# Router logits of a mixture of experts computed with the weights stationary, and an order of work changed with them

## The chip, the core and the metric

The kernel runs on one core of a Trainium2 chip. Its engines work side by side and meet only at semaphores: TensorE (PE, with its weight loads shown apart as PEld), VectorE (DVE), ScalarE (ACT), GpSimd (POOL) and the DMA queues, of which SyncE (SP) issues many. The metric is the time of one execution in microseconds (us), lower is better.

## The reference

A graph layer, a linear attention and a mixture of experts follow each other over 3125 tokens of 256 features. What the change touches is the router at the head of the experts:

```python
logits = tokens @ router_w.T                 # (3125, 256) x (256, 8), float32
probs = softmax(logits); rw, re = top_k(probs, 2); rw = rw / rw.sum(-1)
out = tokens
for e in range(8):
    out = out + combine[:, e:e+1] * (gelu(tokens @ w1[e] + b1[e]) @ w2[e] + b2[e])
```

The tokens here are the layer-normalised sum of the input, the graph layer and the attention.

## The kernel before

The 3125 tokens are 25 tiles of 125 rows, handled in 5 groups of 5 tiles. After the graph and attention part (which ends at about 315 us) comes the router stage, and after that the experts, in 64 chunks of 128 rows that each belong to one expert: 32 chunks for the tokens' first choice (rank 0), 32 for their second (rank 1). A token's row reaches its place in the table of chunks (`xs`, in DRAM) by an indirect DMA that GpSimd issues, one for each tile and rank: `send(t, r2)`, 25 for rank 0 and 25 for rank 1. SyncE loads the first chunk only when all 25 rank 0 sends have landed, and the padding rows of all eight experts too (`store_pad`, issued by SyncE and ScalarE once the counts are known).

The order of work is written out by hand, one program for each engine. For group g:

- TensorE: `graph3(g)` (the last product of the graph layer, five matmuls), `transpose_tokens(g)`, `logits(g)`, `positions(g)` (places of the tokens in their experts' lists).
- VectorE: `add_graph(g)` (adds the graph layer's result, then the variance, signalled as `var2_done`), `scale(g)`, `choose(g)` (the two best experts), `weigh(g)` (the places, signalled as `slot_done`).
- ScalarE: `token_scale(g)` (a square root, with a table load ahead of it for all groups but two), `normalize_tokens(g)`, an exponential for the two weights, `copy_tokens(g)` (transposed tokens out of PSUM).
- GpSimd: for each group, after its `slot_done`, five rank 0 sends and `BETWEEN` rank 1 sends; behind the last group's five, rank 1 sends up to number `EARLY`; the remaining rank 1 sends go between the experts' stores.

VectorE's loop matters for the change and is left as it is by it:

```python
for g in range(G):
    if g + 1 < G:
        scale(g + 1)
    choose(g)
    if g + 2 < G:
        add_graph(g + 2)
    weigh(g)
```

`add_graph(g)` begins by waiting for `graph3(g)`, `positions(g)` on TensorE waits for `weigh(g - 1)`, and `scale(g)` waits for `token_scale(g)`, which waits for `add_graph(g)`.

Of the kernel before, what the change touches and what calls it, by code (L numbers as in the profile page):

```python
# [14 lines left out]
TP = 125  # L15
NT = N // TP
J = 5
G = NT // J
EC = NE // TP
P = 128  # L20
H1, H2 = 64, 32
NX = 8
# [14 lines left out]
NBLK = len(BLOCKS)  # L37
HALF_TILES = 12
MC = 32
BETWEEN, EARLY = 2, 15  # L40
XB = 6
NCH = 2 * MC
CAP = N + P + 3
# [1 line left out]
RR = NX * CAP + NULLS * P  # L45
NOWHERE = 4096.0
CTX0 = 128
assert NG == NB * TP and GT * W == TP and NE % TP == 0


def build(nc, a, out):
# [3 lines left out]
    with ExitStack() as ctx:  # L55
# [3 lines left out]
        def sem(name):  # L59
            return ctx.enter_context(nc.semaphore(name))  # L60
# [4 lines left out]
        lg_ps = bank[3]  # L65
# [4 lines left out]
        den_ps = h0[0:TP, CB:CB + NH]  # L70
        by_token = [y0[0:TP, 0:D], y1[0:TP, 0:D], spare[0:TP, 0:D], y0[0:TP, D:2 * D], y1[0:TP, D:2 * D]]
        pos_ps = h1
        xt_ps, hid_ps, y_ps = (y0, y1), (m0, m1), (h0, h1)

        class Region:
# [18 lines left out]
        r = Region("region_z", NT * H1 + NT * 3 * H1 // 2)  # L94
# [4 lines left out]

        r = Region("region_q", NT * 2 * TP)  # L100
        qp_all = r.take(P, NT * 2 * TP).rearrange("p (t n) -> p t n", t=NT)

        r = Region("region_a", GT * (KW + P) + 2 * NT * P + 2)
        koh = r.take(P, 2 * GT * KW, BF16).rearrange("p (s c n) -> p s c n", s=2, c=GT)
# [20 lines left out]
        tkT = r.take(P, 4 * J * TP).rearrange("p (s k n) -> p s k n", s=2, k=2)  # L125
# [15 lines left out]
        r = Region("region_w", NX * WROW)  # L141
# [11 lines left out]
        r = Region("region_c", 3 * WROW + 3 * D // 2 + 260)  # L153
# [17 lines left out]
        rw = sb("rw", [P, 2, NX])  # L171
# [4 lines left out]
        ident = sb("ident", [P, P])  # L176
# [56 lines left out]
        lg = sb("lg", [TP, J, NX])  # L233
# [22 lines left out]
        edges_in, z_in, gnn_in, q_in, kv_in, mix_in, ffn_in = map(sem, (  # L256
            "edges_in", "z_in", "gnn_in", "q_in", "kv_in", "mix_in", "ffn_in"))
# [19 lines left out]
        summed, agg_ready = map(sem, ("summed", "agg_ready"))  # L277
# [9 lines left out]
        t3_ready, tkT_done, lg_ready, lg_read, diff_done, ex_done, oh_done, pos_ready, pos_read = map(sem, (  # L287
            "t3_ready", "tkT_done", "lg_ready", "lg_read", "diff_done", "ex_done", "oh_done", "pos_ready", "pos_read"))
# [5 lines left out]
        added = [sem(f"added{s}") for s in range(4)]  # L294
        xt_ready, xT_done, w_copied, hid_ready, gelu_done, y_ready, ys_done = map(sem, (
            "xt_ready", "xT_done", "w_copied", "hid_ready", "gelu_done", "y_ready", "ys_done"))
        passed, restored = sem("passed"), sem("restored")

        def column(tile):
# [106 lines left out]
        def _(pool):  # L406
# [130 lines left out]
            for b in range(NB):  # L537
                pool.wait_ge(rows_in[b], 16)
                pool.wait_ge(wins_landed[b], 16)

            def send(t, r2):
                nc.gpsimd.indirect_dma_start(xs, bass.IndirectOffsetOnAxis(slot_i[:, t, r2:r2 + 1], 0),  # L542
                                             rows[:, t, :], None).then_inc(sent[r2], 16)
# [28 lines left out]
        def _(act):  # L572
# [76 lines left out]
            def token_scale(g):  # L649
                act.wait_ge(var2_done, g + 1)  # L650
                nc.scalar.activation(std2[:, g % 2, :], mv2[:, g % 2, :, 1], ACT.Sqrt, bias=epsc[:]).then_inc(std2_done, 1)
# [6 lines left out]

            def copy_tokens(g):
                if g >= 2:  # L660
                    act.wait_ge(lg_ready, g - 1)
                act.wait_ge(t3_ready, g + 1)
                for k, ps in enumerate((m0, m1)):
                    nc.scalar.copy(tkT[:, g % 2, k, 0:4 * TP], ps[:, 0:4 * TP]).then_inc(tkT_done, 1)
                nc.scalar.copy(tkT[:, g % 2, :, 4 * TP:5 * TP], h0[:, 0:CB].rearrange("p (k n) -> p k n", k=2)
                               ).then_inc(tkT_done, 1)

            token_scale(0)
            normalize_tokens(0)
            copy_tokens(0)  # L670
            token_scale(1)
            for g in range(G):
                if g + 1 < G:
                    normalize_tokens(g + 1)
                act.wait_ge(diff_done, g + 1)
                nc.scalar.activation(ex[:], ex[:], ACT.Exp).then_inc(ex_done, 1)
                if g + 1 < G:
                    copy_tokens(g + 1)
                if g + 2 < G:
                    token_scale(g + 2)  # L680
            act.wait_ge(rows_known, 1)
# [26 lines left out]
        def _(dve):  # L708
# [184 lines left out]
            for c in range(2):  # L893
                heads = slice(c * NH // 2, (c + 1) * NH // 2)
                last = nc.vector.tensor_scalar(ksum_of[:, c, heads],
                                               same_head[:].rearrange("p (h a) -> p h a", a=HD)[:, :, 0],
                                               ksum[:, c:c + 1], None, ALU.mult)
# [68 lines left out]
            def chain(ins):  # L966
                link(ins)
# [28 lines left out]

            def choose(g):
                dve.wait_ge(lg_ready, g + 1)
                nc.vector.tensor_copy(lg[:].rearrange("p j x -> p (j x)"), lg_ps[0:TP, 0:J * NX]).then_inc(lg_read, 1)
                dve.wait_ge(lg_read, g + 1)  # L1000
                for j in range(J):
                    last = nc.vector.max(top[:, j, :], lg[:, j, :])
                chain(last)
                for j in range(J):
                    nc.vector.max_index(top_at[:, j, :], top[:, j, :], lg[:, j, :])
                nc.vector.tensor_tensor(ex[:], top[:, :, 1], top[:, :, 0], ALU.subtract).then_inc(diff_done, 1)
                dve.wait_ge(diff_done, g + 1)
                chain(nc.vector.tensor_copy(top_atf[:], top_at[:, :, 0:2]))
                if g >= 1:
                    dve.wait_ge(pos_ready, g)  # L1010
                for r2 in range(2):
                    last = nc.vector.tensor_tensor(oh[:, :, r2, :], iota_x[:],
                                                   top_atf[:, :, r2:r2 + 1].to_broadcast([TP, J, NX]), ALU.is_equal)
                last.then_inc(oh_done, 1)
# [42 lines left out]
            for r2 in range(2):  # L1057
                last = nc.vector.tensor_tensor(upto[:, r2, :, :], up_to[:], nch[:, r2:r2 + 1, :].to_broadcast([1, NX, NX]),
                                               ALU.mult)
            chain(last)  # L1060
            chain(nc.vector.tensor_reduce(ends[:], upto[:], AX_X, ALU.add))
            for r2 in range(2):
                last = nc.vector.tensor_tensor(past[:, r2, :, :], ends[:, r2:r2 + 1, :].to_broadcast([1, MC, NX]),
                                               chunk_of[:].rearrange("p (c a) -> p c a", a=1).to_broadcast([1, MC, NX]),
                                               ALU.is_le)
            chain(last)
            chain(nc.vector.tensor_reduce(expert_f[:], past[:], AX_X, ALU.add))
            for r2 in range(2):
                last = nc.vector.tensor_tensor(past[:, r2, :, :], past[:, r2, :, :],
                                               ends[:, r2:r2 + 1, :].to_broadcast([1, MC, NX]), ALU.mult)  # L1070
# [51 lines left out]
        def _(pe):  # L1122
# [57 lines left out]
            for t in range(NT):  # L1180
# [9 lines left out]
                if t == 14:  # L1190
                    pe.wait_ge(row_done, 1)
                    pe.wait_ge(value_done, 1)
                    for b in range(4):
                        last = nc.tensor.transpose(spare[:, b * TP:(b + 1) * TP], value[:, b, :], ident[0:TP, 0:TP])
# [76 lines left out]
            for t in range(-1, NT + 1):  # L1271
                if t == 0:
                    pe.wait_ge(mix_in, 32)
                    pe.wait_ge(ctx_back, 1)
                    for c in range(2):
                        last = nc.tensor.matmul(mix_ps[:, c * D:(c + 1) * D], mout[:, 0, c * P:(c + 1) * P], wp[:, c, :],
                                                start=True, stop=True)
# [49 lines left out]
            def graph3(g):  # L1327
                if g == 0:
                    pe.wait_ge(h2_act, 1)
                elif g == 1:  # L1330
                    pe.wait_ge(h2_act, 2)
                    pe.wait_ge(h2_dve, 2)
                if g >= 1:
                    pe.wait_ge(x2_done, g * J)
                for j in range(J):
                    q, at = quad_of(g * J + j)
                    nc.tensor.matmul(by_token[j], h2T[q, at * TP:(at + 1) * TP], w3g[q, :],
                                     start=True, stop=True).then_inc(g3_ready, 1)
# [11 lines left out]
            def logits(g):  # L1350
                pe.wait_ge(tkT_done, (g + 1) * 3)
                if g == 0:
                    pe.wait_ge(ffn_in, 16)
                else:
                    pe.wait_ge(lg_read, g)
                for j in range(J):
                    for k in range(2):
                        last = nc.tensor.matmul(lg_ps[0:TP, j * NX:(j + 1) * NX], tkT[:, g % 2, k, j * TP:(j + 1) * TP],  # L1358
                                                rw[:, k, :], start=(k == 0), stop=(k == 1))
                last.then_inc(lg_ready, 1)  # L1360

            def positions(g):
                pe.wait_ge(oh_done, g + 1)
# [15 lines left out]
            graph3(1)  # L1379
            transpose_tokens(0)  # L1380
            logits(0)
            for g in range(G):
                if g + 2 < G:
                    graph3(g + 2)
                if g + 1 < G:
                    transpose_tokens(g + 1)
                positions(g)
                if g + 1 < G:
                    logits(g + 1)
            pe.wait_ge(lg_read, G)  # L1390
            nc.tensor.matmul(lg_ps[0:1, 0:2 * NX], ones16[0:TP, 0:1], cum[:], start=True, stop=False)
            for j in range(J):
# [71 lines left out]
```

## Time and profile before

| | before |
|---|---|
| median of 3 runs | 547.89 us (546.22 to 548.82) |
| the profiled execution | 550.5 us, with a span of 548.8 us |
| TensorE busy / VectorE / ScalarE / GpSimd | 454.5 / 335.5 / 268.6 / 226.4 us |
| mean granted TensorE clock | 0.877 of full speed |

The span runs from the first to the last instruction that the profiler recorded; 1.7 us lie around it. Busy times are unions over each engine. The stage that the change touches lies between 320 and 400 us, in which TensorE's granted clock is 0.50 of full speed from 325 us on.

### The profile page before, as it was taken

How to read it: one execution, taken by the hardware profiler on the slowest of the kernel's cores; microseconds unless marked ns; L12 is line 12 of the kernel's file. 1: busy time of each engine (PE TensorE's matmuls, PEld its weight loads, DVE VectorE, ACT ScalarE, POOL GpSimd, SP SyncE). 2: the span in 40 equal slices, each digit the busy share in tenths (PEclk: the TensorE clock that was granted, in tenths of full speed). 3: DMA queues.
4: the chain of work that ended last, by engine and by line, in shares of the span. 5: the costliest groups of instructions: out<-in, count | busy, mean ns of one | idle time of the engine just before them, and what ended most of it. 6: DMA issues, size and time to landing. Idle time of an engine off the chain costs nothing.

```text
span 548.8 us, 10070 instructions
## 1 busy us (share of the span) xinstructions
PE 454.5 (83%) x3270; PEld 353.6 (64%) x3270; DVE 335.5 (61%) x875; ACT 268.6 (49%) x616; POOL 226.4 (41%) x238
## 2 busy tenths in 40 slices
PE   2799596797899999859999838984079999999993
PEld 1688475686466655526555527874069899999992
DVE  3655756845566677717775165775328788766661
ACT  1375342354577776527777155671034444444440
POOL 4123882737200000000000000677757774487785
PEclk9899888898599999969999885555569999999997
DMA  9605210900546665575676400233656654267762
GB/s 214 151 2 159 73 25 0 306 4 1 119 110 131 121 121 128 122 140 120 122 130 134 96 2 1 62 90 93 161 146 178 173 166 125 78 111 123 117 98 27
DMA packets 122430, 58.72 MB, mean 107 GB/s; under 512 B 95777, under 2 KB 119565, under 8 KB 122378
## 3 DMA queue, kind: packets, MB, share of 16 engines
q1 hardware_dynamic: 107242, 42.29, 33.2%
q0 software_dynamic: 13744, 14.39, 12.6%
q10 hardware_dynamic: 1392, 1.39, 1.0%
q8 instruction: 27, 0.44, 0.4%
q14 instruction: 25, 0.20, 0.1%
HBM read 19.14 MB, written 20.34 MB: 72 GB/s over the span
## 4 chain that ended last, share of the span: by engine, by line
PE 54%; DMA 12%; POOL 11%; issue 8%; DVE 8%; ACT 4%; SPq 2%; POOLq 0%; DVEq 0%; ACTq 0%
PE bank L1226 11%; PE bank L1215 8%; DMA region_a<-region_a 6%; POOL out L560 6%; PE bank L1413 6%; PE bank L1424 5%; PE bank L1257 4%; POOL xs L542 3%; PE bank L1151 3%; DMA rows<-in_x 2%; PE bank L1358 2%; PE bank L1161 2%; PE bank L1164 2%; PE bank L1347 2%; PE bank L1402 2%
## 5 line engine op out<-in xcount | busy, mean ns | idle before, releaser
L624 ACT CAST region_a<-bank 128x500 bf16<-128x500 f32 (+1 forms) x175 | 112.0, 667 | 61.3 <-PE bank L1215 46.5
L1226 PE MATMUL bank<-region_a,region_z 125*64 125x500 bf16 (+1 forms) x525 | 74.6, 382 | 11.5 <-DMA region_a<-region_a 11.5
L542 POOL DMA_INDIRECT xs<-rows,slot_i x50 | 60.3, 1206 | 55.8 <-issue 51.6
L520 POOL COPY wide<-den 125x256 f32<-125x256 f32 x25 | 13.1, 525 | 155.1 <-DVE den L912 155.1
L1215 PEld LDWEIGHTS bank<-region_a 128*128 128x128 bf16 x625 | 42.9, 105 | 48.4 <-issue 31.8
L1215 PE MATMUL bank<-region_a 128*128 128x125 bf16 x625 | 67.8, 230 | 4.5 <-ACT region_a L624 2.0
L1413 PE MATMUL bank<-region_a,region_c 128*128 128x128 f32 x512 | 70.0, 280 | 0.2
L1424 PE MATMUL bank<-region_c,region_a 128*128 128x256 f32 x256 | 65.7, 379 | 0.0
L1413 PEld LDWEIGHTS bank<-region_a,region_c 128*128 128x128 f32 x512 | 63.9, 196 | 1.2 <-issue 0.8
L560 POOL DMA_INDIRECT out<-region_a x32 | 52.1, 1627 | 15.5 <-issue 12.8
L1086 DVE COPY region_c<-region_w 128x1026 f32 x64 | 46.2, 721 | 20.1 <-issue 20.1
L697 ACT ACTIVATE region_a<-bank,region_c 128x128 f32<-128x128 f32 x128 | 40.1, 365 | 35.7 <-PE bank L1413 35.6
L689 ACT COPY region_a<-bank 128x256 f32<-128x256 f32 x64 | 23.9, 373 | 59.2 <-PE bank L1402 58.1
L832 DVE TENSOR_TENSOR region_a<-iota,keys 128x3150 bf16<-128x3150 bf16 x25 | 47.2, 1889 | 0.1
L1226 PEld LDWEIGHTS bank<-region_a,region_z 125*64 125x64 bf16 x525 | 25.5, 113 | 32.6 <-DMA region_a<-region_a 12.5
L838 DVE TENSOR_TENSOR region_a<-iota,locs 128x3200 bf16<-128x3200 bf16 x25 | 46.5, 1858 | 0.0
L1424 PEld LDWEIGHTS bank<-region_c,region_a 128*128 128x128 f32 x256 | 43.7, 190 | 4.1
L1402 PE MATMUL bank<-ident,region_a 128*128 128x128 f32 x128 | 25.2, 280 | 22.1 <-DMA region_a<-xs 22.1
L557 POOL DMA_INDIRECT out<-region_a x32 | 32.7, 1021 | 22.5 <-DVE region_a L1105 16.4
L918 DVE TENSOR_TENSOR qn<-bank,region_q 128x250 f32<-128x250 f32 x25 | 10.5, 419 | 46.7 <-PE bank L1237 44.5
L460 POOL TENSOR_SCALAR rows<-rows,rstd,shift 125x256 f32<-125x256 f32 x25 | 18.7, 748 | 47.1 <-DVE region_a L737 47.0
L1402 PEld LDWEIGHTS bank<-ident,region_a 128*128 128x128 f32 x128 | 18.1, 144 | 28.8 <-issue 21.3
(214 smaller groups left out, 810.6 us busy)
## 6 DMA issues: line engine op xcount, KB each, us to landing
region_a<-xs SPq DMA_DIRECT2D x64, 130.5 KB, 2.6
region_w<-in_w SPq DMA_DIRECT2D x4, 1024.0 KB, 8.8
rows<-in_x SPq DMA_DIRECT2D x5, 560.0 KB
xs<-null SPq DMA_DIRECT2D x2, 913.5 KB, 8.3
xs<-null SPq DMA_DIRECT2D x12, 130.5 KB, 2.8
ztab<-region_z SPq DMA_DIRECT2D x1, 1171.9 KB
out<-region_a POOLq DMA_INDIRECT x64
xs<-rows,slot_i POOLq DMA_INDIRECT x50, 3.9
```

The lines of the kernel that those rows point to most:

```text
L542: nc.gpsimd.indirect_dma_start(xs, bass.IndirectOffsetOnAxis(slot_i[:, t, r2:r2 + 1], 0), rows[:, t, :], None).then_inc(sent[r2], 16)
L560: nc.gpsimd.indirect_dma_start(out, to, ys[:, c % 4, :], None, bounds_check=N - 1, oob_is_err=False, compute_op=ALU.add).then_inc(added[c ...
L624: nc.scalar.copy(to, chunk_ps[n % 2][:, 0:w * TP].rearrange("p (c t u) -> p c t u", c=w, t=NT)).then_inc(adj_done, 1)
L697: last = nc.scalar.activation(hT[:, c % 2, f * P:(f + 1) * P], hid_ps[c % 2][:, f * P:(f + 1) * P], ACT.Gelu, bias=wc[:, c % 3, 4 * D + f: ...
L832: nc.vector.tensor_tensor(koh[:, t % 2, :, :].rearrange("p c (m u) -> p c m u", u=2), counting(KW), columns(keys, t, KW), ALU.is_equal).th ...
L838: nc.vector.tensor_tensor(loh[:, t % 2, :, :].rearrange("p c (m u) -> p c m u", u=2), counting(P), columns(locs, t, P), ALU.is_equal).then ...
L1086: nc.vector.tensor_copy(wc[:, c % 3, :].rearrange("p (a f) -> p a f", a=1), w_all[:, bass.ds(e, 1), :])
L1215: last = nc.tensor.matmul(chunk_ps[n % 2][:, (c - lo) * TP:(c - lo + 1) * TP], loh[:, t % 2, c, :], koh[:, t % 2, c, 0:TP], start=True, st ...
L1226: last = nc.tensor.matmul(block_out(b), zparts[:, t, part, :], adjT[0:TP, t % 2, lo:hi, 0:TP], start=False, stop=False, skip_group_check=True)
L1402: last = nc.tensor.transpose(xt_ps[c % 2][:, k * P:(k + 1) * P], xch[:, c % XB, k * P:(k + 1) * P], ident[:])
L1413: last = nc.tensor.matmul(hid_ps[c % 2][:, f * P:(f + 1) * P], wc[:, c % 3, k * D + f * P:k * D + (f + 1) * P], xT[:, c % 2, k * P:(k + 1) ...
L1424: last = nc.tensor.matmul(y_ps[c % 2][:, 0:D], hT[:, c % 2, f * P:(f + 1) * P], wc[:, c % 3, (2 + f) * D:(3 + f) * D], start=False, stop=( ...
```

## The change

The logits are computed the other way round. Before, each tile's transposed tokens were the stationary operand (a weight load of 125 columns) and the router's 8 columns moved: ten matmuls a group, with the result by token. Now the router's weights, padded with zeros, are stationary, and the tokens move: for the first four tiles of a group 32 columns of weights each, written to four groups of 32 PSUM partitions, and for the fifth tile all 128 columns. The result is by expert, so ScalarE copies it out of PSUM (`copy_logits`) and TensorE turns it back with two transposes (`turn_logits`). GpSimd prepares the padded weights once. Besides, `graph3(g + 2)` moves for g from 1 on, and one rank 1 tile instead of two is sent with each group.

```diff
-BETWEEN, EARLY = 2, 15
+BETWEEN, EARLY = 1, 14
...
+            pool.wait_ge(agg_ready, 1)
+            nc.gpsimd.memset(rw_wide, 0.0).then_inc(rw_zeroed, 1)
+            pool.wait_ge(ffn_in, 16)
+            pool.wait_ge(rw_zeroed, 1)
+            nc.gpsimd.tensor_copy(rw_wide[:, :, 0:NX], rw[:]).then_inc(rw_widened, 1)
...
+            def copy_logits(g):
+                act.wait_ge(lgT_ready, g + 1)
+                if g >= 1:
+                    act.wait_ge(lg_ready, g)
+                nc.scalar.copy(lgT[:], lgT_ps).then_inc(lgT_done, 1)
...
             token_scale(0)
             normalize_tokens(0)
             copy_tokens(0)
+            copy_logits(0)
             token_scale(1)
             for g in range(G):
...
                 if g + 1 < G:
                     copy_tokens(g + 1)
+                    copy_logits(g + 1)
                 if g + 2 < G:
                     token_scale(g + 2)
...
             def logits(g):
                 pe.wait_ge(tkT_done, (g + 1) * 3)
                 if g == 0:
-                    pe.wait_ge(ffn_in, 16)
+                    pe.wait_ge(rw_widened, 1)
                 else:
+                    pe.wait_ge(lgT_done, g)
+                for k in range(2):
+                    for j in range(J - 1):
+                        nc.tensor.matmul(lgT_ps[j * 32:(j + 1) * 32, 0, :], rw_wide[:, k, 0:32],
+                                         tkT[:, g % 2, k, j * TP:(j + 1) * TP], start=(k == 0), stop=(k == 1))
+                for k in range(2):
+                    last = nc.tensor.matmul(lgT_ps[:, 1, :], rw_wide[:, k, :], tkT[:, g % 2, k, (J - 1) * TP:J * TP],
+                                            start=(k == 0), stop=(k == 1))
+                last.then_inc(lgT_ready, 1)
+
+            def turn_logits(g):
+                pe.wait_ge(lgT_done, g + 1)
+                if g >= 1:
                     pe.wait_ge(lg_read, g)
-                for j in range(J):
-                    for k in range(2):
-                        last = nc.tensor.matmul(lg_ps[0:TP, j * NX:(j + 1) * NX], tkT[:, g % 2, k, j * TP:(j + 1) * TP],
-                                                rw[:, k, :], start=(k == 0), stop=(k == 1))
-                last.then_inc(lg_ready, 1)
+                nc.tensor.transpose(lg_ps[0:TP, 0:P], lgT[:, 0, :], ident[:])
+                nc.tensor.transpose(lg_ps[0:TP, P:P + 32], lgT[0:32, 1, :], ident[0:32, 0:32]).then_inc(lg_ready, 1)
...
             logits(0)
+            turn_logits(0)
             for g in range(G):
-                if g + 2 < G:
-                    graph3(g + 2)
+                if g == 0:
+                    graph3(2)
                 if g + 1 < G:
                     transpose_tokens(g + 1)
                 positions(g)
                 if g + 1 < G:
                     logits(g + 1)
+                if 1 <= g and g + 2 < G:
+                    graph3(g + 2)
+                if g + 1 < G:
+                    turn_logits(g + 1)
```

How it moves instructions shows best in the order of each engine. First TensorE before the change, from the end of `positions(0)`: the logits of group 1 (L1358), `graph3(3)` (L1337), the transposes of group 2 (L1347), and the first matmul of `positions(1)` (L1368).

```order
L1374 MATMUL bank<-cum,ones 125x80
L1358 MATMUL bank<-rw,region_a 125x8 [waits lg_read,tkT_done]
L1358 MATMUL bank<-rw,region_a 125x8 x9
L1337 MATMUL bank<-w3g,region_z 125x256 [waits x2_done]
L1337 MATMUL bank<-w3g,region_z 125x256 x4
L1347 MATMUL bank<-ident,rows 128x125 [waits tkT_done,tk_done]
L1347 MATMUL bank<-ident,rows 128x125 x9
L1368 MATMUL bank<-oh,before 125x80 [waits pos_read,cum_done,oh_done]
```

The same place after the change, where L1379 and L1382 are the logits of group 1, L1390 and L1391 their two transposes, L1368 the transposes of group 2 and L1399 the head of `positions(1)`:

```order
L1405 MATMUL bank<-cum,ones 125x80
L1379 MATMUL bank<-region_a,region_q 32x125 [waits lgT_done,tkT_done]
L1379 MATMUL bank<-region_a,region_q 32x125 x7
L1382 MATMUL bank<-region_a,region_q 128x125 x2
L1390 MATMUL bank<-ident,region_q 125x128 [waits lg_read,lgT_done]
L1391 MATMUL bank<-ident,region_q 125x32
L1368 MATMUL bank<-ident,rows 128x125 [waits tkT_done,tk_done]
L1368 MATMUL bank<-ident,rows 128x125 x9
L1399 MATMUL bank<-oh,before 125x80 [waits pos_read,cum_done,oh_done]
```

`graph3(3)` is gone from this place. Further down TensorE's program, from the end of `positions(1)` on, after the change, with the logits of group 2 first:

```order
L1405 MATMUL bank<-cum,ones 125x80
L1379 MATMUL bank<-region_a,region_q 32x125 [waits lgT_done,tkT_done]
L1379 MATMUL bank<-region_a,region_q 32x125 x7
L1382 MATMUL bank<-region_a,region_q 128x125 x2
L1358 MATMUL bank<-w3g,region_z 125x256 [waits x2_done]
L1358 MATMUL bank<-w3g,region_z 125x256 x4
L1390 MATMUL bank<-ident,region_q 125x128 [waits lg_read,lgT_done]
L1391 MATMUL bank<-ident,region_q 125x32
L1368 MATMUL bank<-ident,rows 128x125 [waits tkT_done,tk_done]
```

Here L1358 is `graph3(3)`: it has moved from behind the logits of group 1 to behind those of group 2, and `graph3(4)` in the same way to behind those of group 3. Last, ScalarE after the change, from the exponential of group 0 to that of group 1; L676 and L677 are `copy_tokens(1)`, L684 is the new `copy_logits(1)`, L663 is `token_scale(2)` and L668 `normalize_tokens(2)`:

```order
L695 ACTIVATE ex<-ex 125x5 [waits diff_done]
L676 COPY region_a<-bank 128x500 [waits t3_ready]
L676 COPY region_a<-bank 128x500
L677 COPY region_a<-bank 128x2x125
L684 COPY region_q<-bank 128x250 [waits lg_ready,lgT_ready]
L663 ACT_TABLE_LOAD
L663 ACTIVATE std<-mv,epsc 125x5 [waits var2_done]
L668 ACTIVATE rows<-region_a,shift,rstd 125x256 [waits shift2_done]
L668 ACTIVATE rows<-region_a,shift,rstd 125x256 x4
L695 ACT_TABLE_LOAD
```

One copy is new, and it stands, with its wait for TensorE's logits, ahead of the table load and square root of the next group.

## Rows read from the trace of the kernel before

**Rows 1.** The head of the profile's page.
```profile
span 548.8 us, 10070 instructions
```
**Rows 2.** Chain that ended last, 330 to 394 us: start us, us, what.
```profile
332.46 4.37 PE bank L1358 x20
...
342.52 4.37 PE bank L1358 x20
346.89 2.00 PE bank L1337 x10
...
393.34 3.85 DMA xs<-rows,slot_i
```
**Rows 3.** Timeline of sends, slots and last logits: start us, us, instruction [idle before].
```profile
344.11 0.17 DVE L1029 CAST slot_i<-slot_f 125x10 int32<-125x10 f32 x1
345.30 1.26 POOL L542 DMA_INDIRECT xs<-rows,slot_i  x1 [40.90 <-issue]
354.24 0.17 DVE L1029 CAST slot_i<-slot_f 125x10 int32<-125x10 f32 x1
364.37 0.17 DVE L1029 CAST slot_i<-slot_f 125x10 int32<-125x10 f32 x1
371.92 4.37 PE L1358 MATMUL bank<-rw,region_a 128*125 128x8 f32 x20 [0.87 <-ACT region_a L665]
380.29 0.58 DVE L1029 CAST slot_i<-slot_f 125x10 int32<-125x10 f32 x1
```
**Rows 4.** Timeline of one group's steps, 338 to 354 us.
```profile
338.90 1.75 DVE L974 SCALAR_TENSOR_TENSOR region_a<-bank,rows 125x256 f32<-125x256 f32 x5
340.57 1.72 DVE L978 BATCH_NORM_STATS2 stats<-region_a 125x6 f32<-125x256 f32 x5
342.32 0.45 DVE L983 BATCH_NORM_AGGREGATE mv<-stats 125x2 f32<-125x6 f32 x5
345.16 2.56 ACT L656 ACTIVATE rows<-region_a,shift,rstd 125x256 f32<-125x256 f32 x5 [1.08 <-DVE shift L994]
348.82 2.35 PE L1347 MATMUL bank<-ident,rows 125*128 125x125 f32 x10
351.26 1.05 ACT L664 COPY region_a<-bank 128x500 f32<-128x500 f32 x2 [2.01 <-PE bank L1347]
352.20 0.39 ACT L665 COPY region_a<-bank 128x250 f32<-128x250 f32 x1
352.60 1.28 ACT L651 ACT_TABLE_LOAD   x1
353.90 0.30 ACT L651 ACTIVATE std<-mv,epsc 125x5 f32<-125x5 f32 x1
```
**Rows 5.** SyncE queue's waits, 330 to 420 us: total us, times, longest us.
```profile
SPq L393 <- DMA xs<-null: 4.9, 1, 4.9
...
SPq L394 <- DMA xs<-rows,slot_i: 4.5, 1, 4.5
```
**Rows 6.** Timeline of packed matmuls.
```profile
241.94 1.46 PE L1226 MATMUL bank<-region_a,region_z 125*64 125x500 bf16 x6
...
315.08 0.85 PE L1125 MATMUL bank<-zeros 128*128 128x500 bf16 x4
...
317.80 1.74 PE L1318 MATMUL bank<-region_a,w2g 64*32 64x125 f32 x50 [1.87 <-ACT region_a L638]
```
**Rows 7.** Windows: busy us of each engine, PEclk, DMA share, GB/s.
```profile
241.00:245.00 4.00, 4.00 (x24) 1.41 (x20) 0.00 (x0) 1.45 (x2) 0.00 (x0) 0.50 0.53 124
315.00:316.00 1.00, 0.94 (x6) 0.29 (x3) 0.42 (x1) 0.03 (x1) 0.00 (x0) 1.00 0.00 0
317.50:319.50 2.00, 1.70 (x50) 1.49 (x50) 0.25 (x1) 0.70 (x3) 0.00 (x0) 1.00 0.04 8
350.00:360.00 10.00, 9.13 (x47) 8.13 (x46) 7.78 (x49) 6.96 (x12) 8.17 (x7) 0.50 0.33 87
```
**Rows 8.** Timeline of GpSimd's first store of an expert's chunk.
```profile
409.26 1.08 POOL L557 DMA_INDIRECT out<-region_a  x1 [4.29 <-DVE region_a L1105]
```

More of the change, by code:

```diff
@@ L47 @@
 CTX0 = 128
+LGT0 = 192
 assert NG == NB * TP and GT * W == TP and NE % TP == 0
@@ L72, in build @@
         pos_ps = h1
+        lgT_ps = lg_ps[:, LGT0:LGT0 + 2 * P].rearrange("p (s n) -> p s n", s=2)[:, :, 0:TP]
         xt_ps, hid_ps, y_ps = (y0, y1), (m0, m1), (h0, h1)
@@ L101, in build @@
         qp_all = r.take(P, NT * 2 * TP).rearrange("p (t n) -> p t n", t=NT)
+        r.restart()
+        rw_wide = r.take(P, 2 * P).rearrange("p (k n) -> p k n", k=2)
+        lgT = r.take(P, 2 * TP).rearrange("p (s n) -> p s n", s=2)
         r = Region("region_a", GT * (KW + P) + 2 * NT * P + 2)
@@ L296, in build @@
             "xt_ready", "xT_done", "w_copied", "hid_ready", "gelu_done", "y_ready", "ys_done"))
+        rw_zeroed, rw_widened, lgT_ready, lgT_done = map(sem, ("rw_zeroed", "rw_widened", "lgT_ready", "lgT_done"))
         passed, restored = sem("passed"), sem("restored")
@@ L660, in copy_tokens @@
                 if g >= 2:
-                    act.wait_ge(lg_ready, g - 1)
+                    act.wait_ge(lgT_ready, g - 1)
                 act.wait_ge(t3_ready, g + 1)
@@ L998, in choose @@
                 dve.wait_ge(lg_ready, g + 1)
-                nc.vector.tensor_copy(lg[:].rearrange("p j x -> p (j x)"), lg_ps[0:TP, 0:J * NX]).then_inc(lg_read, 1)
+                nc.vector.tensor_copy(lg[:], lg_ps[0:TP, 0:J * 32].rearrange(
+                    "p (j x) -> p j x", j=J)[:, :, 0:NX]).then_inc(lg_read, 1)
                 dve.wait_ge(lg_read, g + 1)
```

## The prediction, made before the changed kernel ran

> **What bounds the kernel now.** I read the chain that ended last first, then the timeline of the router stage that it leads through, then the waits of SyncE's queue, because the experts' first load hangs there. The sum is made against the profiled execution: a span of 548.8 us [rows 1] inside 550.5 us, 2.6 us over the median of 547.89, and the difference is carried over to the median.
>
> Until 345 us the chain is TensorE's logits and what feeds them, 4.37 us for a group [rows 2]. Then it is GpSimd. Its first send starts at 345.30, right after the first slots (344.11 + 0.17), and the last rank 0 send, which is number 33 with two rank 1 sends after each of the first four groups, starts at 393.34 [rows 2, 3]. That is 48.04 us over 32 steps, 1.50 us each, the pace of an issuing engine that is never idle. The slots of groups 1 to 4 are ready at 354.41, 364.54, 372 and 380.46 [rows 3]; GpSimd comes to them at about 345.3 plus 7, 14, 21 and 28 sends, 355.8, 366.3, 376.7 and 387.2. So each group is ready before it is asked for, group 2 by only 1.8 us and group 4 by 6.8 us. The last rank 0 send lands at 393.34 + 3.85 = 397.19 and the experts start behind it. SyncE's queue confirms it: it waits 4.9 us for the padding and then another 4.5 us for the sends [rows 5], so the padding landed at about 392.7.
>
> Two limits thus lie close together: GpSimd's count of sends, and the pace at which groups come, 10.1 us from slot to slot (344.28, 354.41, 364.54). That pace is TensorE's own: logits 4.37, `graph3` 2.00, transposes 2.35, and ScalarE's copies 1.05 and 0.39 less their overlap of 0.11, 10.05 us with no gap in between [rows 2, 4]. The granted clock is 0.50 there [rows 7], 1.2 of 2.4 GHz.
>
> **The change part by part.** *The logits.* The 20 records of a group (two for each float32 matmul) become 16 with 32 columns of weights in four column groups, and 4 with 128. For the 16 the nearest row is the second graph layer's matmuls, with 125 moving columns in three column groups: 50 records in 1.74 us at full clock, 35 ns each [rows 6, 7], so 70 ns at half clock and 1.1 us for 16. The 4 others move 125 columns as a transpose does, 0.235 us each (2.35 for 10) [rows 4]: 0.94 us. With a quarter microsecond, a guess, for filling and for changing the shape of the array, I take 2.3 us. Bounds: 4 column groups that share fully give a quarter of 16 x 0.235, so 1.9 us with the four; no sharing at all gives 16 x 0.235 + 0.94 = 4.7 us. That 128 rows don't hinder sharing is in the aggregation's rows: six matmuls of 500 columns in two column groups, 125 rows each, take 1.46 us at half clock [rows 6, 7], 0.49 us for a pair, where four of 500 columns that can't share take 0.85 us at full clock [rows 6, 7], 0.21 each and so 0.42 at half. So I stay near the low end.
>
> *The turn.* A ScalarE copy of 250 columns, 0.39 us [rows 4], and two transposes at 0.235 plus filling, 0.85 us together (between 0.5 and 1.2). With handovers of 0.04 us the logits of a group come 1.3 us after TensorE's matmuls, so for the first group 2.3 + 1.3 stands against 4.37.
>
> *The order on ScalarE.* The copy stands before the next square root, so that root now waits for the logits. Before, table load, root, VectorE's scale and the normalisation ran beside the 4.37 us of logits. After: L(1), the logits' end of group 1, then copy 0.43, load 1.30, root 0.30, scale 0.60, normalisation 2.56, transposes 2.39, copies 1.40, and L(2) after 2.3 more [rows 4], handovers counted in: 11.3 us for a group and not 10.1. The first two groups escape: `token_scale(1)` has no table load, and the transposes of group 1 start where they do now, at about 338.8. So L(0) ends at 332.46 + 2.3 = 334.8, L(1) at 342.5 + 2.3 = 344.8, L(2) at 356.1. Before, L(0) and L(1) ended at 336.8 and 346.9 [rows 2] and L(2) one pace later, at 357.0, so up to here the change is ahead by 0.9 us.
>
> *The later `graph3`.* This is the costly part. `graph3(3)` now follows the logits of group 2. VectorE's program asks for it in `add_graph(3)`, which stands ahead of `weigh(1)`, ahead of `scale(3)`, ahead of the normalisation and transposes of group 3. So the steps that overlapped form one line: L(2) end, `graph3` 2.00 and a handover of 0.1, `add_graph` 3.87 (338.90 to 342.77), `weigh` and `scale` 2.40 (to 345.16), normalisation 2.56, transposes 2.39, copies 1.40, logits 2.3 [rows 2, 4]. That makes 17.0 us. `choose(2)` and `positions(2)` fit beside normalisation and transposes. L(3) ends at 373.1, L(4), by the same line with `graph3(4)`, at 390.1, where it ended at 371.92 + 4.37 = 376.29 before [rows 3].
>
> *GpSimd's slots.* `weigh(2)` stands behind `add_graph(4)`, which waits for `graph3(4)` behind L(3): 373.1 + 2.1 + 3.87 + 1.5 (342.77 to 344.28 in the rows) = 380.6 for the slots of group 2, 16 us late. From there GpSimd has six sends for group 2, six for group 3 and four before the last rank 0 send: 16 x 1.50 = 24.0 us, start at 404.6, landed at 408.45. Group 4's slots come at L(4) + 1.3 + 4.2 (376.29 to 380.46) = 395.6, before GpSimd wants them at 398.6. The padding follows the counts by 15.1 us, 392.7 to 407.8, which is 0.6 us before the sends. The experts start 408.45 - 397.19 = **11.3 us later**.
>
> *One rank 1 tile a group.* Four sends fewer ahead of the last rank 0 send are worth 4 x 1.50 = 6.0 us while GpSimd is never idle. Here it idles ahead of groups 1 and 2, and only the two sends fewer of groups 2 and 3, 3.0 us, are in the sum above. Ten rank 1 sends now follow the last rank 0 one instead of seven. They end 11 steps, 16.5 us, behind its start; the first expert's store comes 15.9 us behind it (393.34 to 409.26) after 4.29 us of idling [rows 2, 8]. Half a microsecond late, with four result buffers, costs nothing; without that cover it would be 0.5 us. GpSimd's two new instructions run in its 40.90 us of idling [rows 3]: nothing.
>
> Sum, by another way: GpSimd comes to group 2 at 380.6 instead of 366.3, 14.3 us later, and has 16 instead of 18 steps from there to the last rank 0 send, 3.0 us less: **+11.3 us**.
>
> *A rule weighed against it.* Rows say that loads and matmuls of packed tiles overlap: PEld was busy 1.49 of the 1.70 us that PE was [rows 7]. The Trainium skill ("TensorE: Matmul & The Clock Gate", Part 3, what overlaps and what doesn't) says that a weight load overlaps running matmuls only where its row group differs; all eight new matmuls use all rows. By that rule each of the 16 records would pay for its own load, and the forecast would be 563 us (below, worked out from rows). The trace speaks more for the overlap, since most of those 50 used one half of the rows.
>
> **Rivals.** *Column groups don't share, or loads stand between them* (8%). Unshared, L is 4.7, each of L(0) to L(3) adds 2.4, and the slots of group 2 come 9.6 us later still: 568.8 us. With a load of 30 ns per record (1.49 us over 50, 60 at half clock) paid on top, L is 3.3 and the time 563 us. Against it are the pairs of rows 6. *GpSimd falls behind in the experts* (9%): the extra sends contend with the first loads, or the half microsecond grows with 11 instead of 10 sends between stores, 1 to 3 us more, 561 us. *The other side: GpSimd's count decides* (5%). If the moved `graph3` didn't lengthen the pace, the four sends fewer would be the change: 6.0 us, cut to 4.5 by the padding, which lands at 392.7 [rows 5], so 543.4 us. It decides if slots of group 2 are ready by 345.3 + 12 x 1.50 = 363.3, a pace of 9.5 us or less. The 17 us line speaks against it, and each wait in it is in the program. *Little change* (3%): the two effects cancel, which takes a pace of about 11.5 us, as if `graph3` had stayed.
>
> **How the numbers follow.** The main case has 75%: 547.9 + 11.3 = 559.2 us. L from 1.9 to 2.9 moves it by -1.6 to +2.4 (four logits stand ahead of the slots of group 2), the turn by less than 1 through the padding, and a run's scatter by 1.3. That is 556 to 563; with the late GpSimd and half of the loads' case I give 555 to 565. Half a percent, 2.7 us, is about what a measurement here can tell from no change. Faster 5%, same 3%, slower 92%.
>
> **What would show it.** In the changed profile: logits matmuls of some 2.3 us a group; ends of logits near 335, 345, 356, 373 and 390; VectorE idle before `add_graph(3)` until `graph3` has run, some 2 us behind the logits; GpSimd idle for about 9 us before the slots of group 1 and again before those of group 2 near 380; the last rank 0 send near 404.6 and SyncE's first load near 409. The prediction is wrong if slots keep a pace of 10 us, if the padding lands well after the sends, or if the experts' stage itself (397 us to the end) changes its length.

## The result, and the profile after the change

The changed kernel takes 557.18 us (median of 4 runs, 554.05 to 559.09) where the kernel before takes 547.06 us (4 runs, 545.69 to 548.82): a ratio of 1.0161, with a 95% interval of 1.0116 to 1.0206. A second comparison, with 6 runs, gave 1.0245 (1.0185 to 1.0306), 559.37 us against 547.43. Ratios, here and below, leave out runs more than 1.5% above the fastest of the same kernel, and medians are over all runs. The prediction said 559.2 us, in a range of 555 to 565.

The head of the page after, which answers to [rows 1]:

```profile
span 557.4 us, 10105 instructions
PE 446.3 (80%) x3279; PEld 341.3 (61%) x3280; DVE 335.4 (60%) x875; ACT 270.3 (49%) x621; POOL 228.2 (41%) x240
```

TensorE works 8 us less than before and the kernel ends later, so what was added on it is waiting. The absolute times of the router stage lie 2.84 us lower than in the first profile: the first router transposes start at 325.86 here and at 328.70 there. The same code ahead of that point put them between 320.9 and 328.8 us over all profiles of this study, so I compare stages from that start on, and call "router stage" the time from there to SyncE's first load of an expert's chunk. It was 69.3 us before and is 81.4 us now.

The timeline of the group that pays, after the change (start us, us, instruction, idle time before it and what ended it), which answers to [rows 4]; rows between these are left out. L1379 and L1382 are the logits of group 2, L1358 is `graph3(3)`, L994 the head of `add_graph(3)`, L1050 the slots of group 1, L668 `normalize_tokens(3)`, L1368 the transposes of group 3:

```profile
350.68 1.06 PE L1379 MATMUL bank<-region_a,region_q 128*32 128x125 f32 x16 [0.87 <-ACT region_a L677]
351.67 1.22 PE L1382 MATMUL bank<-region_a,region_q 128*128 128x125 f32 x4
352.82 2.07 PE L1358 MATMUL bank<-w3g,region_z 32*125 32x256 f32 x10
355.03 1.75 DVE L994 SCALAR_TENSOR_TENSOR region_a<-bank,rows 125x256 f32<-125x256 f32 x5 [8.81 <-PE bank L1358]
358.45 0.44 DVE L1003 BATCH_NORM_AGGREGATE mv<-stats 125x2 f32<-125x6 f32 x5
360.24 0.17 DVE L1050 CAST slot_i<-slot_f 125x10 int32<-125x10 f32 x1
361.29 2.56 ACT L668 ACTIVATE rows<-region_a,shift,rstd 125x256 f32<-125x256 f32 x5 [2.06 <-DVE shift L1014]
363.91 2.35 PE L1368 MATMUL bank<-ident,rows 125*128 125x125 f32 x10 [8.17 <-ACT rows L668]
366.34 1.05 ACT L676 COPY region_a<-bank 128x500 f32<-128x500 f32 x2 [0.97 <-PE bank L1368]
367.72 1.06 PE L1379 MATMUL bank<-region_a,region_q 128*32 128x125 f32 x16 [0.87 <-ACT region_a L677]
```

Read it downwards as one line: each step starts when the one before it ends, with less than 0.1 us of overlap anywhere. VectorE had stood idle for 8.81 us before `graph3(3)` let it go, and TensorE for 8.17 us before ScalarE's normalisation let it go. From the logits of group 2 to those of group 3 it takes 367.72 - 350.68 = 17.04 us, where TensorE before was idle for only 0.87 us of a pace of 10.1 us, while it waited for ScalarE's copies. The next group repeats it, 384.77 - 367.72 = 17.05.

What reaches GpSimd and the experts, timeline after the change (a selection), for [rows 3]:

```profile
341.62 1.26 POOL L554 DMA_INDIRECT xs<-rows,slot_i  x1 [27.72 <-DVE slot_i L1050]
361.31 1.19 POOL L554 DMA_INDIRECT xs<-rows,slot_i  x1 [10.94 <-DVE slot_i L1050]
377.28 0.17 DVE L1050 CAST slot_i<-slot_f 125x10 int32<-125x10 f32 x1
378.35 1.18 POOL L554 DMA_INDIRECT xs<-rows,slot_i  x1 [8.40 <-DVE slot_i L1050]
384.90 0.58 DVE L1050 CAST slot_i<-slot_f 125x10 int32<-125x10 f32 x1
392.35 0.57 DVE L1050 CAST slot_i<-slot_f 125x10 int32<-125x10 f32 x1
```

GpSimd, which before left only 0.30 us between one send and the next, now waits 10.94 us for the slots of group 1 and 8.40 for those of group 2. From 378.35 on it sends every 1.50 us until the last rank 0 send. The chain that ended last shows that send, and SyncE's waits (total us, times, longest) show the landings, for [rows 2] and [rows 5]:

```profile
402.34 3.92 DMA xs<-rows,slot_i
```
```profile
SPq L399 <- DMA xs<-null: 5.6, 1, 5.6
...
SPq L400 <- DMA xs<-rows,slot_i: 1.2, 1, 1.2
```

The padding was 4.5 us ahead of the sends before (4.2 in a second profile of that kernel) and is 1.2 us ahead now. That distance isn't steady: the second profile of the changed kernel has it at 3.7 us.

```profile
SPq L399 <- DMA xs<-null: 4.4, 1, 4.4
SPq L400 <- DMA xs<-rows,slot_i: 3.7, 1, 3.7
```

In all profiles of this study the sends landed last, behind the padding. The windows of the stage (busy us of PE, PEld, DVE, ACT, POOL, granted clock, DMA share, GB/s) show the same clock, 0.50, and a TensorE that is half idle or more in the last two, for [rows 7]:

```profile
330.00:340.00 10.00, 8.14 (x60) 6.35 (x56) 6.95 (x44) 5.95 (x12) 0.00 (x0) 0.50 0.01 2
350.00:360.00 10.00, 5.06 (x32) 3.25 (x32) 4.76 (x21) 2.57 (x5) 0.36 (x1) 0.50 0.08 22
370.00:380.00 10.00, 2.78 (x12) 1.59 (x12) 7.48 (x46) 3.58 (x7) 1.34 (x2) 0.50 0.06 18
```

### The profile page after: what moved, and what is told of

Read it like the earlier page. It is cut to its first block, busy times and chain, and to the rows that moved or that the text cites. A ratio compares the mean times of both kernels' runs of the same rounds, so it can differ in the third digit from the quotient of the medians.

```text
span 557.4 us, 10105 instructions
## 1 busy us (share of the span) xinstructions
PE 446.3 (80%) x3279; PEld 341.3 (61%) x3280; DVE 335.4 (60%) x875; ACT 270.3 (49%) x621; POOL 228.2 (41%) x240
## 3 DMA queue, kind: packets, MB, share of 16 engines
q0 software_dynamic: 13744, 14.39, 12.2%
## 4 chain that ended last, share of the span: by engine, by line
PE 52%; DMA 11%; POOL 10%; issue 9%; DVE 8%; ACT 6%; SPq 2%; POOLq 1%; DVEq 0%; ACTq 0%
PE bank L1247 10%; PE bank L1236 8%; DMA region_a<-region_a 6%; PE bank L1449 6%; POOL out L572 5%; PE bank L1460 5%; POOL xs L554 3%; PE bank L1278 3%; PE bank L1172 3%; PE bank L1182 3%; DMA rows<-in_x 2%; PE bank L1185 2%; ACT rows L668 2%; PE bank L1368 2%; PE bank L1258 1%
## 5 line engine op out<-in xcount | busy, mean ns | idle before, releaser
L1449 PEld LDWEIGHTS bank<-region_a,region_c 128*128 128x128 f32 x512 | 63.8, 196 | 1.6 <-issue 1.2
L1172 PE MATMUL bank<-wzkv,region_a 128*125 128x320 f32 x100 | 34.5, 471 | 0.0
```

The costliest lines, as they stand in the source:

```text
L1172: last = nc.tensor.matmul((y0, y1)[s][0:TP, 0:H1 + D], xnT[:, s, k, :], wzkv[:, k, 0:H1 + D], start=(k == 0), stop=(k == 1))
L1449: last = nc.tensor.matmul(hid_ps[c % 2][:, f * P:(f + 1) * P], wc[:, c % 3, k * D + f * P:k * D + (f + 1) * P], xT[:, c % 2, k * P:(k + 1) ...
```

## The experiments

Theory A is the prediction's: `graph3` behind the next logits puts `graph3`, `add_graph`, `weigh`, `scale`, the normalisation, the transposes, the copies and the logits in one line. Rival B is that the new logits themselves, with their copy and their turn back, are the cost. A third reading, that ScalarE's order (the copy of the logits ahead of the next square root) is the cost, goes with them. The runs came in three sets, each on one chip with the kernel before beside it: e1 to e4 on what is called the second chip, e5, e6, e8 and e9 on the third, e7 and e10 to e12 on the fourth. On the second chip the kernel before took 559.55 us; on the others 547 to 548. "Changed" is the changed kernel; e1, e2, e3, e6, e7, e10, e11 and e12 are edits of it, e4 and e5 of the kernel before.

| kernel | ratio to before, 95% interval | median us | router stage us | from first load to end us |
|---|---|---|---|---|
| before, first profile | | 547.06 | 69.3 | 150.8 |
| changed | 1.0161 [1.0116, 1.0206] | 557.18 | 81.4 | 150.1 |
| e8, before again | (one run) | 546.5 | 69.1 | 151.1 |
| e9, changed again | 1.0245 [1.0185, 1.0306] | 559.37 | 81.8 | 150.3 |
| e5, before with the late `graph3` alone | 1.0323 [1.0267, 1.0378] | 564.59 | 86.8 | 152.5 |
| e6, changed, two rank 1 tiles again | 1.0306 [1.0256, 1.0356] | 564.27 | 85.1 | 151.4 |
| e1, changed, `graph3` back | 0.9929 [0.9899, 0.9958] | 554.36 | 69.0 | 158.2 |
| e12, the same again | 0.9988 [0.9958, 1.0019] | 545.59 | 70.1 | 149.2 |
| e3, changed, ScalarE's order put right | 1.0101 [1.0044, 1.0159] | 563.29 | 79.0 | 158.4 |
| e4, before with fewer sends alone | 0.9923 [0.9883, 0.9963] | 552.64 | 65.5 | 159.7 |
| e2, changed, both orders put right | 0.9840 [0.9800, 0.9881] | 550.14 | 63.8 | 160.1 |
| e10, the same again | 0.9878 [0.9823, 0.9933] | 540.19 | 63.8 | 150.3 |
| e11, the same, two rank 1 tiles | 0.9973 [0.9927, 1.0018] | 546.22 | 69.1 | 150.7 |
| e7, changed, one column group | (one run) | 563.87 | 88.9 | 150.2 |

The router stage and the time behind it come from one profiled execution of each kernel. For e9 a slowdown of 1.9 to 2.2% was expected and a stage 12.2 us longer; it was 2.45% slower, with both ends of that expectation inside the interval, and the stage 12.7 us longer than e8's.

**e5_graph3_late_only**: the kernel before with the late `graph3` alone.

```diff
-                if g + 2 < G:
-                    graph3(g + 2)
+                if g == 0:
+                    graph3(2)
                 if g + 1 < G:
                     transpose_tokens(g + 1)
                 positions(g)
                 if g + 1 < G:
                     logits(g + 1)
+                if 1 <= g and g + 2 < G:
+                    graph3(g + 2)
```

> The kernel before with the late graph3 alone: old logits, two rank 1 tiles. Theory A: two steps of 19.3 us instead of 10.2, the slots of group 2 come 18.1 us later, experts start 16.7 us later, +3.0% (564 where before takes 547). Rival B (the new logits and their turn are the cost): within 2 us of before.

The old logits with the moved `graph3` are slower than the whole change, by 3.2%, and the router stage grows by 17.5 us over the first profile of before and 17.7 over e8, against 16.7 expected. The timeline:

```profile
353.91 1.75 DVE L974 SCALAR_TENSOR_TENSOR region_a<-bank,rows 125x256 f32<-125x256 f32 x5 [10.98 <-PE bank L1337]
...
359.12 0.17 DVE L1029 CAST slot_i<-slot_f 125x10 int32<-125x10 f32 x1
...
373.11 1.75 DVE L974 SCALAR_TENSOR_TENSOR region_a<-bank,rows 125x256 f32<-125x256 f32 x5 [10.97 <-PE bank L1337]
378.32 0.17 DVE L1029 CAST slot_i<-slot_f 125x10 int32<-125x10 f32 x1
```

The step between slots is 19.20 us, the 17.05 of the changed kernel plus the 2.15 by which the old logits (4.37) are longer than the new (2.22). The late `graph3` alone, without the new logits, costs more than the whole change, which Rival B doesn't allow. (The 0.9 us over what was expected is the time from the slots of group 2 to GpSimd's first send, which the part on the prediction comes back to.)

**e1_graph3_back and e12_graph3_back_again**: the changed kernel with `graph3` where it was.

```diff
-                if g == 0:
-                    graph3(2)
+                if g + 2 < G:
+                    graph3(g + 2)
                 if g + 1 < G:
                     transpose_tokens(g + 1)
...
-                if 1 <= g and g + 2 < G:
-                    graph3(g + 2)
```

> The changed kernel with the graph3 of each group back where it was before, ahead of the transposes. Theory A (the late graph3 put five steps in line): TensorE's logits end about 11.2 us apart in every group, no 17 us gaps, the experts start about 12.5 us earlier than in the changed kernel and 1.3 us earlier than in the kernel before, 546 us. Rival B (the new logits and their turn cost it, wherever graph3 is): the time stays near 557.

> The same kernel as e1_graph3_back, on another chip. Router stage 69.0 us there, level with before; the whole ran 3.9 us faster on that chip. If the router stage is all, this one is within 0.3% of before here.

The router stage falls by about 12 us, to 69.0 and 70.1, level with before, and slots come 11.2, 11.1 and 10.7 us apart. With e5 this rules Rival B out. The expected gain of 1.3 over before was not there: the stage stood at -0.3 and +0.8. Counted from the router's first transposes, the last rank 0 send did start 0.9 and 1.1 us earlier than before. The gain was lost behind it: from the start of that send to the experts' first load it took 5.3 and 6.5 us, against 4.7 and 4.5 in the two profiles of the kernel before. In e12 it is the landing, 5.66 us where [rows 2] has 3.85; why it took longer isn't shown.

```profile
388.24 5.66 DMA xs<-rows,slot_i
```

Level with before doesn't mean that nothing is lost any more. GpSimd still idles for 2.0 to 2.4 us ahead of the slots of groups 1, 2 and 3, which uses up what the fewer sends give. What ScalarE's order costs there shows in e2.

**e3_scale_first_only**: the changed kernel with `token_scale` ahead of `copy_logits`.

```diff
                 if g + 1 < G:
                     copy_tokens(g + 1)
-                    copy_logits(g + 1)
                 if g + 2 < G:
                     token_scale(g + 2)
+                if g + 1 < G:
+                    copy_logits(g + 1)
```

(`token_scale(1)` and `copy_logits(0)` change places as well.)

> The changed kernel with ScalarE's order alone put right, graph3 still late. Theory A: only the step from the logits of group 1 to those of group 2 gets shorter (11.2 to 9.0 us), the two steps of 17.1 stay, so it gains 2.7 us and stays 8.6 us above before, near 554.5. If ScalarE's order were the cause of the slowdown, it would be near 547 or below.

The router stage is 79.0 us, 2.4 and 2.8 less than in the two profiles of the changed kernel against 2.7 expected. The first step between slots falls from 19.8 to 17.05 us, the next stays (slots ready at 335.64, 352.69, 369.73). It is 1.0% slower than before. Of this slowdown ScalarE's order is a real but small part.

**e4_sends_only**: `BETWEEN, EARLY = 1, 14` in the kernel before, nothing else.

> The kernel before with one rank 1 tile a group alone. GpSimd never idles there, so the last rank 0 send starts 4.5 us earlier (slots of group 2 hold it by 1.4 of the 6.0), and the padding, landed at 392.7, then comes level: experts start 4.3 us earlier, 542.8 us. Rival: what is taken out ahead comes back in the experts' stage, where one more send stands between the stores, and the time stays at 547.

It is 0.8% faster, 4.3 us of 559.55, and the router stage is 3.6 to 3.8 us shorter, of the 6.0 that four sends are worth. The timeline shows where the rest went, and SyncE's waits (total us, times, longest) what came last:

```profile
360.51 1.19 POOL L542 DMA_INDIRECT xs<-rows,slot_i  x1 [1.70 <-issue]
...
382.94 1.65 POOL L542 DMA_INDIRECT xs<-rows,slot_i  x1 [0.30 <-issue]
```
```profile
SPq L393 <- DMA xs<-null: 6.1, 1, 6.1
SPq L394 <- DMA xs<-rows,slot_i: 1.3, 1, 1.3
```

GpSimd idled for 1.70 instead of 0.30 us before the first send of group 2, whose slots weren't ready (1.4 us, as expected), and one send took 1.65 us instead of 1.19. The last rank 0 send started 4.3 us earlier, and from it to the load it took 5.1 us against 4.7 and 4.5. The padding, 4.5 us ahead of the sends before, is 1.3 ahead here: the next limit, but not the one that was met. The whole gained as much as the stage, within its interval, so what was taken out ahead doesn't come back later.

**e6_two_rank1_again**: the changed kernel with `BETWEEN, EARLY = 2, 15`.

> The changed kernel with two rank 1 tiles a group again. GpSimd idles ahead of groups 1 and 2, so only the tiles of groups 2 and 3 count: 2 x 1.5 = 3.0 us later than the changed kernel. Rival: GpSimd's slack swallows them, 0 us.

The router stage is 3.3 to 3.6 us longer than in the two profiles of the changed kernel: two sends, at 1.50 each, and a little. GpSimd's idle time ahead of groups 1 and 2 swallows the others: it is 9.42 and 6.88 us, 1.5 less each than the 10.94 and 8.40 of the changed kernel.

**e2_graph3_back_scale_first and e10_best_again**: both orders put right, the edits of e1 and e3 together.

> As the last one, and ScalarE takes the next group's square root ahead of the copy of the logits. Theory A with its second part (the copy holds the square root, 11.2 us a group): the pace falls to 9.4 us, GpSimd's sends decide again, the experts start 6.7 us earlier than before, 540.5 us. If ScalarE's order is worth nothing, it ends at the last one's time.

> The same kernel as e2_graph3_back_scale_first (graph3 back, ScalarE's square root ahead of the copy of the logits), on another chip. The router stage measured 63.8 us there against 69.1 and 69.3 before, 5.4 less, while the whole ran 8.8 us faster. If the router stage is all that differs, a chip with an experts' stage of 151 us shows 5.4 us, 1.0%; if the second chip's 1.6% is general, 8.8 us.

This beats both kernels: 0.9840 on the second chip and 0.9878 on the fourth, there 540.19 us against 548.28. The router stage is 63.8 us twice, 5.3 to 5.5 shorter than before, where 6.7 had been worked out. The last rank 0 send starts 5.9 to 6.0 us earlier, and from it to the load it takes 0.3 to 0.8 us longer. The fourth chip's ratio (1.2% is 6.7 us) has 5.4 us within its interval; the second chip's has not (1.6%, at least 6.6 us of 559.55), and what else it holds is open (below). Against e1 and e12 the stage is 5.1 and 6.3 us shorter, so ScalarE's order is worth that much once `graph3` is back in its place, about twice what it is worth in e3. The timeline of GpSimd in e10 shows what decides:

```profile
356.34 1.19 POOL L554 DMA_INDIRECT xs<-rows,slot_i  x1 [0.30 <-issue]
358.40 1.19 POOL L554 DMA_INDIRECT xs<-rows,slot_i  x1 [0.87 <-DVE slot_i L1051]
359.89 1.19 POOL L554 DMA_INDIRECT xs<-rows,slot_i  x1 [0.30 <-issue]
```

From its first send to the last rank 0 one it is held up by slots only here, for 0.87 instead of 0.30 us. It is GpSimd's count of sends again.

**e11_best_two_rank1**: the last one with `BETWEEN, EARLY = 2, 15`, so the new logits alone in a good order.

> As the last one with two rank 1 tiles a group, so the new logits alone, in a good order. GpSimd never idles then, and its 33 sends decide again: only the first slots come earlier, by 0.8 us. Theory A: 0.8 us faster than before, within 0.5%. Rival: the logits' shorter work is worth itself, 2 us a group and so some 5 us.

0.9973, an interval that holds no change, and a router stage of 69.1 us as before. GpSimd isn't held up by slots once. Shorter logits are worth nothing while GpSimd is never idle; together with the sends they let the slots keep up with a faster GpSimd: the stage is 65.5 us with fewer sends alone (e4) and 63.8 with both.

**e7_one_column_group**: the changed kernel, the eight narrow matmuls all into the first 32 partitions.

```diff
-                        nc.tensor.matmul(lgT_ps[j * 32:(j + 1) * 32, 0, :], rw_wide[:, k, 0:32],
-                                         tkT[:, g % 2, k, j * TP:(j + 1) * TP], start=(k == 0), stop=(k == 1))
+                        nc.tensor.matmul(lgT_ps[0:32, 0, :], rw_wide[:, k, 0:32],
+                                         tkT[:, g % 2, k, j * TP:(j + 1) * TP], start=True, stop=True)
```

> The changed kernel with all eight narrow matmuls of a group written to the first 32 partitions, each started and stopped by itself, so that they can't share the array; the logits are then not those of the reference, and the routing differs, so only the router stage is to be read. Sharing is real: the 16 records take 16 x 0.21 = 3.4 us instead of 1.06, the logits 4.5 instead of 2.2, and the stage grows by 10 us. If the columns never shared, nothing changes.

In the timeline:

```profile
337.14 3.10 PEld L1379 LDWEIGHTS bank<-region_a,region_q 128*32 128x32 f32 x16 [1.22 <-ACT region_a L677]
337.14 3.54 PE L1379 MATMUL bank<-region_a,region_q 128*32 128x125 f32 x16 [1.11 <-ACT region_a L677]
340.62 1.22 PE L1382 MATMUL bank<-region_a,region_q 128*128 128x125 f32 x4
```

The 16 records take 3.54 us instead of 1.06, 3.3 times as long, and the four wide ones 1.22 as ever. So four column groups do share the array, at 128 rows each. The logits of a group take 4.7 us here (337.14 to 341.84), the bound that the prediction gave for no sharing. The stage grew by 7.2 to 7.5 us rather than 10. The windows show why: at times the clock was granted at its upper level, where the changed kernel has 0.50 throughout (busy us of PE, PEld, DVE, ACT, POOL, granted clock, DMA share, GB/s, of the kernel with one column group):

```profile
327.00:330.00 3.00, 3.00 (x17) 2.44 (x16) 0.00 (x0) 0.00 (x0) 0.00 (x0) 0.59 0.00 0
330.00:334.00 4.00, 2.13 (x16) 1.42 (x16) 2.60 (x25) 2.77 (x7) 0.00 (x0) 1.00 0.00 0
334.00:338.00 4.00, 2.48 (x21) 2.24 (x22) 3.90 (x18) 3.06 (x6) 0.00 (x0) 0.78 0.02 4
```
```profile
334.41 1.29 PE L1368 MATMUL bank<-ident,rows 125*128 125x125 f32 x10 [1.82 <-ACT rows L668]
...
374.33 1.13 PE L1358 MATMUL bank<-w3g,region_z 32*125 32x256 f32 x10
```

TensorE had been busy for the whole of the first window before it rose. At the upper level the transposes of group 1 took 1.29 us instead of 2.35, and `graph3(4)` 1.13 instead of 2.07. Such shorter records, with the logits that ran at that level, shorten the line by 1.9 us from the logits of group 0 to those of group 1, by 0.4 from group 2 to 3 and by 1.4 from group 3 to 4. That is 3.7 of the 9.9 us that 4 x 2.48 make; 6.2 are left, and the slots of group 2 came 6.4 us later. The rest of the stage's growth lies between the last rank 0 send and the load, 6.2 us instead of 4.9 to 5.0.

## Why the prediction was right, step by step

- *What bounds the kernel.* Right: GpSimd's sends, with the padding 4.5 us behind in rank. e4 (fewer sends alone, -3.6 to -3.8 us in the stage) and e11 (shorter logits alone, nothing) show that it is the sends. The padding comes next, and in no profile did it land last: in e4 it was 1.3 us ahead of the sends.
- *The logits.* 2.3 us forecast, 1.06 + 1.16 = 2.22 measured. 70 ns a record was read from the second graph layer's rows, 66 measured. With every load paid for on top, the prediction's rows made it 3.3 us. The Trainium skill ("TensorE: Matmul & The Clock Gate", Part 3, The mechanism) says that weight loads overlap running matmuls only where the row group differs. The trace disagrees: all eight matmuls use the same rows, and their 16 loads and 16 matmuls ran in 1.06 us together. The trace of e7 shows the loads beside the matmuls too (3.10 of 3.54 us); what the column group decides there is whether the matmuls share the array.
- *The turn.* 0.85 us forecast for the two transposes, 0.92 measured (332.28 to 333.20).
- *The order on ScalarE.* 11.3 us a group forecast, 11.27 measured between the logits of groups 1 and 2 (339.41 to 350.68). e3 shows its worth while `graph3` is late, 2.4 to 2.8 us; e2 and e10 against e1 and e12 its worth without that, 5.1 to 6.3.
- *The later `graph3`.* 17.0 us forecast, 17.04 and 17.05 measured. e5 (put in alone, +17.5 to +17.7 us) and e1 and e12 (taken out, level with before) show from both sides that it is the cause of the slowdown.
- *GpSimd's slots.* The slots of group 2 were forecast 51.9 us after the first router transposes and came after 51.6. The 16 sends took 24.0 us as forecast (378.35 to 402.34). Mis-sized was a term that I took as nothing: an idle GpSimd needs 0.9 us from the slots (377.45) to its first send (378.35). The row of before shows it (344.28 to 345.30) and I counted it there alone. With it, 0.3 us less for the slots, 0.1 more for the landing (3.92) and 0.2 more between landing and load, the stage grows by 12.1 us, not by 11.3.
- *The sum.* +11.3 us forecast; +12.1 and +12.7 in the stage, from the two pairs of profiles; +10.1 (medians, first comparison) and +11.9 (second) for the whole, or by the ratios 1.6 and 2.45% where the forecast is 2.1%. So the two comparisons lie on either side of the forecast, and that the total fits better than the stage is luck. The code ahead of the stage, which is the same, ended up to 8 us apart in the profiles of this study; that this scatter is what parts the two ratios is likely but not shown.
- *One rank 1 tile a group.* Worth 3.0 us within the changed kernel by the forecast, 3.3 to 3.6 by e6. The half microsecond of lateness in the experts that was forecast cost nothing visible: 150.1 to 150.3 us from first load to end, 150.8 and 151.1 before.
- *The side that didn't happen.* The forecast said that GpSimd's count decides if the pace is 9.5 us or less, and gave 543.4 us, 4.5 less than before. e10 has such a pace (slots 9.15 and 9.5 us apart), its stage is 5.3 to 5.5 us shorter than before, and it ran in 540.19. The cut to 4.5 by the padding was too strict there, because the counts come earlier in that kernel as well: the slots of group 4, from which they follow, were ready 3.7 us earlier than before.

What stays open: on the second chip the part behind the first load took 158 to 160 us, on the others 149 to 153, and with the very same kernels (158.2 in e1 against 149.2 in e12, 160.1 in e2 against 150.3 in e10). In all four profiles of the second chip VectorE waited on events that the trace lays to no engine (9.8 us in six waits in e4, 5.7 to 9.7 in e1 to e3; none in e8 or e12), in the half of the experts whose results are written to the output and not yet added to it. The kernel before wasn't profiled on that chip, so how its own 559.55 us divide isn't known, and e1's 0.7% there against 0.1% on the fourth chip may come from it.

## What to carry to other kernels

Before a block is moved in one engine's program, walk down the programs of the engines that wait for it: here `graph3` left TensorE's path free for 2 us, but VectorE had its consumer in front of everything else. A loop over engines is as long as its longest closed line, and a move by one group can turn a step that overlapped into one that is waited for in every turn. Shorter work ahead of an engine that is never idle gives nothing; find that engine (here GpSimd, 1.50 us a send, 33 in a row) and take work from in front of its last needed item, then look at what lies next (here the padding, which landed 4.5 us before the sends). Level with before can hide a loss: e1 lost on ScalarE's order what it gained on sends, and only putting both orders right showed it.

## What the runs showed of the hardware that I had not expected

Four column groups with all 128 rows each and float32 operands share TensorE to 3.3 of a possible 4 times: 66 ns a record at half clock (1.06 us over 16) against 221 (3.54 us over 16) when all go to one column group. An indirect DMA on GpSimd follows the last within 0.30 us when it needn't wait, but after an idle wait it starts 0.9 to 1.0 us behind the event that it waited for (377.45 to 378.35, and 340.62 to 341.62). The last indirect DMA before the load took 3.6 us to land in one profile and 5.7 in another (e8 and e12). And the same two kernels ran their experts' stage at 149 to 150 us on one chip and at 158 to 160 on another.
